# One tile of y made on GpSimd and transposed by DMA, and one of eight weight blocks split on GpSimd

## The reference

```python
x = x + matmul(fake_quant(layernorm(x)), fake_quant(ctx_4096))      # layer 1
y = layernorm(x)                                                    # layer 2
logits = y @ W_router.T
topk_p, topk_i = top_k(softmax(logits), 2)
combine = (one_hot(topk_i) * (topk_p / sum(topk_p))).sum(1)
h = einsum('nd,erd->ner', y, A_stack) * combine[..., None]
x = x + y @ W_base.T + b_base + einsum('ner,eor->no', h, B_stack) * 2.0
```

## Time and profile before

| | before |
|---|---|
| time, median of 3 runs | 168.58 us (168.55 to 169.04) |
| time of the profiled execution | 168.88 us |
| its span, first to last instruction | 167.1 us |
| TensorE busy | 155.1 us, 93% of the span |
| VectorE busy | 127.4 us, 76% |
| ScalarE busy | 72.6 us, 43% |
| GpSimd busy | 37.9 us, 23% |
| mean granted TensorE clock | 0.997 of full speed |

### The profile page before, as it was taken

One profiled execution on the slowest core, in us unless ns is written; L12 is line 12 of the kernel. 1 busy time (PEld: TensorE's weight loads), 2 busy tenths in 40 slices (PEclk: granted clock), 3 DMA queues, 4 the chain that ended last, 5 costly groups with the idle time before them and its releaser, 6 DMA issues.

```text
span 167.1 us, 2467 instructions
## 1 busy us (share of the span) xinstructions
PE 155.1 (93%) x875; PEld 80.5 (48%) x875; DVE 127.4 (76%) x283; ACT 72.6 (43%) x96; POOL 37.9 (23%) x113
## 2 busy tenths in 40 slices
PE   6858889879999999999999999999999999999990
PEld 3324335425446654644564456445644564555540
DVE  7988668999999989999889875988485828607702
ACT  3266699869999873225005300800080008003000
POOL 8204150343000433040614153125300040000000
PEclk9999999999999999999999999999999999999998
DMA  5999999991798523605430903291327002700311
GB/s 100 367 418 409 412 409 408 408 410 63 218 330 263 201 52 74 177 16 158 95 63 4 234 17 63 48 173 34 63 46 205 4 0 44 209 0 0 129 63 65
DMA packets 23677, 26.94 MB, mean 161 GB/s; under 512 B 17776, under 2 KB 18032, under 8 KB 23664
## 3 DMA queue, kind: packets, MB, share of 16 engines
q1 hardware_dynamic: 23520, 26.78, 50.8%
q10 hardware_dynamic: 144, 0.00, 0.0%
HBM read 18.38 MB, written 4.19 MB: 135 GB/s over the span
## 4 chain that ended last, share of the span: by engine, by line
PE 60%; DVE 12%; DMA 10%; ACT 9%; SPq 3%; issue 2%; POOL 2%; DVEq 0%; POOLq 0%
PE ps L889 37%; PE ps L840 10%; DMA xs<-in_x 7%; PE ps L877 6%; ACT w_hi L412 5%; DMA stage<-in_ctx_kv 3%; DVE w_lo L625 2%; SPq L208 2%; PE ps L868 2%; PE ps L870 2%; PE ps L869 2%; ACT a L366 1%; DVE a L556 1%; DVE ar_lo L619 1%; SPq L203 1%
## 5 line engine op out<-in xcount | busy, mean ns | idle before, releaser
L889 PE MATMUL ps<-w_hi,yt_hi 128*128 128x512 f16 x128 | 38.3, 380 | 0.9 <-ACT w_hi L412 0.9
L889 PE MATMUL ps<-w_hi,yt_lo 128*128 128x512 f16 x128 | 38.2, 379 | 0.0
L889 PE MATMUL ps<-w_lo,yt_hi 128*128 128x512 f16 x128 | 37.2, 379 | 0.0
L840 PE MATMUL ps<-a,a_t 128*128 128x512 f16 x128 | 30.1, 379 | 2.2 <-ACT a L366 0.9
L366 ACT ACTIVATE a<-stage,prm,inv_s 128x1024 uint8<-128x1024 f32 x16 | 19.5, 1241 | 9.5 <-DMA stage<-in_ctx_kv 9.2
L447 ACT ACTIVATE gate<-gate,ar_undo 128x1 f32<-128x1 f32 x8 | 2.4, 295 | 46.5 <-DVE gate L661 46.5
L840 PEld LDWEIGHTS ps<-a,a_t 128*128 128x128 f16 x128 | 12.2, 98 | 16.8 <-ACT a L366 1.4
L889 PEld LDWEIGHTS ps<-w_hi,yt_lo 128*128 128x128 f16 x128 | 12.5, 98 | 15.1 <-DVE yt_lo L638 0.2
L889 PEld LDWEIGHTS ps<-w_lo,yt_hi 128*128 128x128 f16 x128 | 12.5, 98 | 14.1
L889 PEld LDWEIGHTS ps<-w_hi,yt_hi 128*128 128x128 f16 x128 | 11.5, 98 | 15.0 <-issue 2.1
L293 POOL TENSOR_SCALAR root<-mvy 128x1 f32<-128x1 f32 x8 | 1.9, 234 | 57.7 <-DVE mvy L514 57.7
(11 more groups left out here) (138 smaller groups left out, 248.1 us busy)
## 6 DMA issues: line engine op xcount, KB each, us to landing
stage<-in_ctx_kv SPq DMA_DIRECT2D x16, 512.0 KB, 5.5
stage<-in_w_t SPq DMA_DIRECT2D x8, 512.0 KB, 13.0
xs<-in_x SPq DMA_DIRECT2D x7, 512.0 KB, 12.0
out_dram<-xs SPq DMA_DIRECT2D x7, 512.0 KB, 3.0
ar_raw<-in_ar_t SPq DMA_DIRECT2D x1, 544.0 KB, 13.7
xs<-in_x SPq DMA_DIRECT2D x2, 256.0 KB, 3.8
b_raw<-in_b_t SPq DMA_DIRECT2D x1, 512.0 KB, 12.5
bias_sb<-in_bias SPq DMA_DIRECT2D x1, 512.0 KB, 13.3
```

The costliest lines, as they stand in the source:

```text
L840: last = nc.tensor.matmul(ps[:, s1_bank(t) + h, :], a1_t[:, t % 4, k, :], a2[:, k, h * H:(h + 1) * H], start=k == 0, stop=k == K - 1)
L889: ins = nc.tensor.matmul(ps[:, OUT_BANK[p] + h, :], part, rhs[:, k, h * H:(h + 1) * H], start=k == 0 and i == 0, stop=stop and i == 2)
```

## The change

Tile 1's y is no longer transposed by TensorE. GpSimd writes it twice, as fp16 (`y_hi`) and as fp32 (`y`); VectorE makes `y_lo` from the two; SP issues two DMA transposes, ahead of the loads of ctx blocks 8 to 15. The two copies out of PSUM (ScalarE L442, VectorE L647) and the eight TensorE transposes of tile 1 go. Behind that GpSimd makes `w_hi` of block 6, which ScalarE no longer makes. The core of the diff:

```diff
+        POOL_W = 6
...
+        def w_hi_made(k):
+            if k == POOL_W:
+                return pool_w_hi_ready, 1
+            return w_hi_ready, k + 1 if k < POOL_W else k
...
             def yt_free(t):
                 if t == 2:
                     sp.wait_ge(ar_done, 2)
-                else:
+                elif t > 2:
                     sp.wait_ge(out_done, t - 1)
...
+            transpose_y_hi(1)
+            transpose_y_lo(1)
             for n in range(K, N):
                 load_ctx(n)
...
-            def make_y(t):
-                pool.wait_ge(y_scaled, t + 1)
-                pool.wait_ge(y_transposed, t)
-                nc.gpsimd.tensor_scalar(y[:, :], xs[:, t, :], y_scale[:, t:t + 1], y_bias[:, t:t + 1], ALU.mult,
+            def make_second_y():
+                pool.wait_ge(y_scaled, 2)
+                nc.gpsimd.tensor_scalar(y_hi[:, :], xs[:, 1, :], y_scale[:, 1:2], y_bias[:, 1:2], ALU.mult,
+                                        ALU.add).then_inc(first_y_hi_ready, 1)
+                pool.wait_ge(y_transposed, 1)
+                nc.gpsimd.tensor_scalar(y[:, :], xs[:, 1, :], y_scale[:, 1:2], y_bias[:, 1:2], ALU.mult,
                                         ALU.add).then_inc(y_ready, 1)
+
+            def split_w(k):
+                pool.wait_ge(w_scale_ready, 1)
+                nc.gpsimd.tensor_scalar(w_hi[:, k, :], stage[:, k, :], scale_w[:, 0:1], None,
+                                        ALU.mult).then_inc(pool_w_hi_ready, 1)
...
-            make_y(1)
+            make_second_y()
+            split_w(POOL_W)
...
             for k in range(K):
-                split_w(k)
-            split_yt(1)
+                if k != POOL_W:
+                    split_w(k)
             split_ar()
...
             sum_x1(3)
+            make_y_lo(1)
             for k in range(4):
                 split_w(k)
-            split_yt(1)
             split_w(4)
             split_ar()
...
-                if k == 2:
+                if k == K // 2 - 1:
                     pe.wait_ge(yt_lo_ready, 1)
-                    transpose_y(1)
             pe.wait_ge(x1_summed, TB)
-            pe.wait_ge(yt_hi_ready, 2)
+            pe.wait_ge(*yt_hi_landed(1))
             for k in range(K):
                 wide(1, k, False, parts=(0,))
-            pe.wait_ge(yt_lo_ready, 2)
+            pe.wait_ge(*yt_lo_landed(1))
```

More of the change, by code:

```diff
@@ L171, in xattn_ffn @@
         ar_hi_ready, ar_lo_ready = sem("ar_hi_ready"), sem("ar_lo_ready")
-        w_hi_ready, w_lo_ready = sem("w_hi_ready"), sem("w_lo_ready")
+        w_hi_ready, pool_w_hi_ready, w_lo_ready = sem("w_hi_ready"), sem("pool_w_hi_ready"), sem("w_lo_ready")
         b_hi_ready, b_lo_ready = sem("b_hi_ready"), sem("b_lo_ready")
@@ L177, in xattn_ffn @@
         yt_hi_ready, yt_lo_ready = sem("yt_hi_ready"), sem("yt_lo_ready")
-        y_hi_ready, y_lo_ready = sem("y_hi_ready"), sem("y_lo_ready")
+        first_y_hi_ready, y_hi_ready, y_lo_ready = sem("first_y_hi_ready"), sem("y_hi_ready"), sem("y_lo_ready")
         yt_hi_in, yt_lo_in = [sem(f"yt_hi_in{i}") for i in range(2)], [sem(f"yt_lo_in{i}") for i in range(2)]
@@ L192, in yt_hi_landed @@
         def yt_hi_landed(t):
-            return yt_hi_in[t % 2], 16 * (t // 2)
+            return yt_hi_in[t % 2], 16 * ((t + 1) // 2)
         def yt_lo_landed(t):
-            return yt_lo_in[t % 2], 16 * (t // 2)
+            return yt_lo_in[t % 2], 16 * ((t + 1) // 2)
+        def w_hi_made(k):
+            if k == POOL_W:
+                return pool_w_hi_ready, 1
+            return w_hi_ready, k + 1 if k < POOL_W else k
         block = stack.enter_context(nc.Block())
@@ L242, in transpose_y_hi @@
                 yt_free(t)
-                sp.wait_ge(y_hi_ready, t - 1)
+                if t == 1:
+                    sp.wait_ge(first_y_hi_ready, 1)
+                else:
+                    sp.wait_ge(y_hi_ready, t - 1)
                 sp.dma_start_transpose(yt_hi[:, t % 2, :, :], y_hi[:, :]).then_inc(yt_hi_in[t % 2], 16)
@@ L247, in transpose_y_lo @@
                 yt_free(t)
-                sp.wait_ge(y_lo_ready, t - 1)
+                sp.wait_ge(y_lo_ready, t)
                 sp.dma_start_transpose(yt_lo[:, t % 2, :, :], y_lo[:, :]).then_inc(yt_lo_in[t % 2], 16)
@@ L420, in make_y_hi @@
                 act.wait_ge(y_scaled, t + 1)
-                if t > 2:
-                    act.wait_ge(*yt_hi_landed(t - 1))
+                act.wait_ge(*yt_hi_landed(t - 1))
+                if t == 2:
+                    act.wait_ge(y_lo_ready, 1)
                 nc.scalar.activation(y_hi[:, :], xs[:, t, :], ACT.Identity, bias=y_bias[:, t:t + 1],
@@ L426, in make_y @@
             def make_y(t):
[L427 to L430, removed]
+                act.wait_ge(y_lo_ready, t - 1)
                 nc.scalar.activation(y[:, :], xs[:, t, :], ACT.Identity, bias=y_bias[:, t:t + 1],
@@ L438, in split_first_yt @@
                                          ps[:, YT_BANKS.start + h, :], ACT.Copy).then_inc(ready, 1)
[L440 to L443, removed]
             def gate_weight(t):
@@ L623, in split_w @@
             def split_w(k):
-                dve.wait_ge(w_hi_ready, k + 1)
+                dve.wait_ge(*w_hi_made(k))
                 nc.vector.scalar_tensor_tensor(out=w_lo[:, k, :], in0=stage[:, k, :], scalar=scale_w[:, 0:1],
@@ L640, in split_first_yt @@
                                             ALU.subtract).then_inc(lo_ready, 1)
[L642 to L648, removed]
-            def make_y_lo(t):
-                dve.wait_ge(y_hi_ready, t - 1)
+            def make_y_lo(t):
+                if t == 1:
+                    dve.wait_ge(first_y_hi_ready, 1)
+                else:
+                    dve.wait_ge(y_hi_ready, t - 1)
+                    dve.wait_ge(*yt_lo_landed(t - 1))
                 dve.wait_ge(y_ready, t + 1)
-                if t > 2:
-                    dve.wait_ge(*yt_lo_landed(t - 1))
                 nc.vector.tensor_tensor(y_lo[:, :], y[:, :], y_hi[:, :], ALU.subtract).then_inc(y_lo_ready, 1)
@@ L925, in _ @@
             for k in range(K):
-                pe.wait_ge(w_hi_ready, k + 1)
+                pe.wait_ge(*w_hi_made(k))
                 wide(0, k, False, parts=(0,))
```

## The result

The changed kernel takes 169.21 us (median of 20 runs, 168.72 to 169.88) against 168.52 us for the kernel before (20 runs): a ratio of 1.0042, 95% interval 1.003 to 1.0054. That is 0.69 us slower where +1.0 was forecast.

What follows compares the result with a forecast made beforehand. VectorE's and ScalarE's lists and the ctx loads were taken to bound the kernel up to `lora(1)`. Exclusion +0.9 and loads +0.1 gave +1.0 on 168.58: 169.6 us, own range 169.3 to 170.1, 8-in-10 range 168.5 to 170.3.

Steps and rivals of the forecast that it cites:

- What bounds the kernel: Before `lora(1)` at 67.87 us the path runs through VectorE, ScalarE and ctx loads; afterwards TensorE works without a gap.
- TensorE's gain of half a microsecond: TensorE reaches tile 1 at 44.8 instead of 45.37 us, 0.5 to 0.6 us earlier, worth nothing.
- the cover: TensorE's 0.37 us wait for `hct_lo` at `lora(1)`, which has to stay for TensorE's earlier arrival to be worth nothing.
- The waits of 1.5 us for `hct_lo`: Expected sign in the changed profile: TensorE waits for `hct_lo` 1.5 us in all where 0.37 was.
- Order on GpSimd and VectorE: At about 40 us GpSimd starts `w_hi` first, at 40.1 to 40.2; VectorE's `y_lo` starts at 41.2 to 41.4.
- The price of exclusion: `y_lo` stands until GpSimd's `w_hi` is through, shifting VectorE's list +0.9 us, or +1.1 if `y_lo` goes first.
- That it goes through to lora(1) nearly whole: A delay of VectorE at 40 us passes through ctx loads, ScalarE and gate to `lora(1)`, nearly whole.
- w_hi on GpSimd at 1.19 us: GpSimd's `w_hi` of block 6 should take about the 1.19 us of L329, running 40.2 to 41.4.
- What the loads add: Five ctx loads (8 to 12) following without pause add +0.1 us, with 0 and +0.5 as bounds.
- Nothing at the end: From `lora(1)` on, the end is its start plus a fixed amount, as the change leaves TensorE's later work alone.
- no exclusion: Rival: `w_hi` under way does not hold up `y_lo`, VectorE's list stays, 168.6 us; chance 0.20.
- GpSimd starved: Rival: from 40.29 us VectorE never lets `w_hi` in, block 6 comes at about 50.2, 176 us; chance 0.03.

Runs made afterwards that it cites:

- a3: Kernel before, with w_hi of block 6 made on GpSimd after waiting for the sum of tile 3; 170.35 us, ratio 1.0099.
- a4: Changed kernel, with GpSimd making w_hi of block 6 twice, one after the other; 172.40 us, ratio 1.0203 to the kernel before.
- a1: Changed kernel, but ScalarE makes all eight w_hi again and GpSimd only the two copies of y; 168.46 us, ratio 0.9978 to the kernel before.
- b2: Kernel before, plus an unused GpSimd instruction that reads a tile of x, started after the sum of tile 3; 169.12 us, ratio 1.003.
- c3: Changed kernel, with a second operation (adding 0.0) in GpSimd's w_hi; 168.90 us, ratio 1.0025 to the kernel before.
- c1: Changed kernel without w_hi on GpSimd, and ScalarE's row sum of tile 0 moved behind y of tile 2; 167.82 us, ratio 0.9943 to before.
- d1: Kernel before, with two more small DMAs on SP behind the load of x tile 7; 168.13 us, ratio 0.9964.
- b1: Kernel before, plus an unused GpSimd fill of 128 x 1024 fp32, started after the sum of tile 3; 168.57 us, ratio 0.9999.
- a2: Kernel before, with w_hi of block 6 made on GpSimd directly behind its y of tile 1; 168.64 us, ratio 0.9987.

## Why the prediction was right, and where it was off

- *What bounds the kernel*: the result held, the reason only in half. TensorE's gain of half a microsecond (44.29 - 37.30 = 6.99 us from the sum of tile 2 to tile 1, 45.37 - 37.91 = 7.46 before) was worth nothing, because VectorE and ScalarE became later than that: TensorE waited 1.40 us for them ahead of `lora(1)`. But the prediction took the 0.37 us at `lora(1)` for the cover under which TensorE could come earlier or later, and that is not what they are. They are the same in every kernel that keeps VectorE's order, also in a3 and a4, where TensorE is the late one. In the kernel before TensorE had no wait from tile 1 to that point (22.11 of 22.13 us busy), and its 1.85 us in a3 came through whole. The waits of 1.5 us for `hct_lo` that the prediction looked for were 0.70, and 1.77 with those for `hc`.
- *Order on GpSimd and VectorE*: held. `w_hi` was first, by 0.12 us.
- *The price of exclusion*, +0.9 on VectorE's list: measured +0.70 against before and +0.84 against a1; in the time 0.75 (a1 to changed, by the medians). A little too high, and near by luck: it was worked out from a row of 1.19 us that is held for its whole length. The row was 2.87, by the same rule +2.6 us, and VectorE was held for only 0.83 of it.
- *That it goes through to lora(1) nearly whole*: it did in the changed kernel (0.71 of 0.84 against a1). In b2, in the old order, only 0.26 of 0.6 arrived in the profile, though the median rose by 0.46.
- *w_hi on GpSimd at 1.19 us*: wrong, 2.87. L329 has two operations and this one has one, and with a second one it takes 1.12 (c3). It did no harm, block 6 came at 42.46 and TensorE began it at 42.56; but that is 0.1 us from a wait.
- *What the loads add*, +0.1 with 0.5 as the upper bound: the term most mis-sized. It is +0.65 at `lora(1)` (a1 against before), and moving the row sum takes 0.60 of it away (c1), which shows that ScalarE's list is the way. That the loads make ScalarE late is read from its waits; part of it is that block 10 also landed more slowly, which no run explains. I counted how late the loads would be and how little ScalarE had to spare, but not that ScalarE works through blocks 10 to 13 and a row sum without a pause once block 10 is late, with the gate behind them in its list.
- *Nothing at the end*: wrong. I had it that the end is `lora(1)` plus a fixed amount. Up to the last sum that is so, 96.20 us before and 96.15 after. From there to the end it is 0.6 us less in the changed kernel, and two more DMAs in SP's list are enough for that (d1). The too small term and the missing one have opposite signs and nearly cancelled; that the +1.0 was nearer than its parts is luck.
- *The rivals*: no exclusion is out (a1, b2). GpSimd starved didn't happen here, but its mechanism is real in part: in a3 and b2 GpSimd stood for two and three of VectorE's instructions, not one. The argument against it, from one cast, did not carry over. Nor do those rows show the other direction for instructions with two sources, as the prediction read them: they are of a fill, and in b1 a fill held up no `w_lo`. That a GpSimd instruction under way does hold up `y_lo` is shown by the changed kernel, by c3 and by a1, in which it is absent.

## What to carry to other kernels

Before work goes to GpSimd, look at what VectorE runs at that moment: beside instructions with two SBUF sources a whole-tile read cost VectorE about 0.8 us, beside ones with a PSUM source or as a mere fill nothing. An engine that is relieved of work but fed by a later transfer does not come earlier, and what stands in its list ahead of something another engine waits for (here a row sum of 1.2 us) becomes the path. And compare profiles from an event the change leaves alone, and at the end too: two spans 0.1 us apart hid +0.7 and +0.66 in the middle, -0.6 at the end and -0.6 at the start.

## What the runs showed of the hardware that was not expected

- GpSimd's instruction over 128 x 1024 took 2.87 us with one operation and 1.12 with two (c3), fp32 in and fp16 out both times; 2.87 was seen in four kernels, and VectorE lost 0.83 us at most beside such a row.
- A GpSimd read that waits for VectorE is not let in at the first boundary between two of VectorE's instructions: it waited for two (a3) and three (b2), where a cast of VectorE got in at once behind GpSimd's fill.
- The last store on SP started 0.40 us after its data in the kernels with the old number of DMAs on SP (62 with the store itself), and 0.02 us after with two more (d1), with an issue of 0.42 us instead of 0.33. Why two DMAs move this, and what one or three would do, was not tried and stays open.
- Why block 10 landed 6.1 us after its issue in the changed kernel, where before it took 4.7 us, is open as well: in a2, with the loads in the old order, block 11 took 6.7, so the transposes ahead of them are not the only cause.
